# Ranks of the second sort's last four parts made in layer 0 instead of the sort, and 392 late scatters for 256, in a graph network kernel

## The chip, the cores and the metric

One core of a Trainium2 chip. The metric is the device time of one execution in microseconds: the median of three runs is 8976.88 us (8976.27 to 8980.71). Below, "POOL" is GpSimd, "DVE" VectorE, "ACT" ScalarE, "PE" TensorE and "SP" SyncE.

## The reference, cut to what matters

The reference runs four graph layers over 6250 nodes of 128 features and 100,000 edges (src, dst), each followed by a residual and a layer norm:

```
x = layernorm(x + L0(x))    mean of x[src] by dst, two 128x128 products, rows scaled to length 1
x = layernorm(x + L1(x))    (x @ weight[type])[src] * edge_weight, summed by dst, relu
x = layernorm(x + L2(x))    5 rounds: segment_sum((h @ W)[src], dst), then a GRU cell; then two dense layers
x = layernorm(x + L3(x))    an MLP on (x[src], x[dst], edge_attr) for each edge, summed by src, MLP on nodes
```

Layers 0 to 2 sum over edges by dst, layer 3 sums by src. So the edges are needed in two orders.

## The kernel before, in words

The work stands in five blocks, one after the other, each with a program for every engine and a barrier at its end: `sort_edges`, `layer0`, `layer1`, `layer2` (five rounds) and `edge_mlp` (layer 3).

**The sort.** Edges lie as 128 partitions by 784 columns. The first order (by dst, for layers 0 to 2) is made by a sorting network of 146 compare stages between 20 turns (numbers 0 to 19), in which the data are transposed, by PE and copies of ACT, alternately to rows (even turns) and to chunks (odd turns). DVE compares and moves (lines 844 to 883), ACT keeps copies (lines 543 to 557). The second order (by src, for layer 3) is a counting sort. For each of 8 parts of 98 columns, DVE makes the rank of each edge inside its tile: ten *rank turns* of five tiles (`rank_turn`, lines 781 to 814), each an equality against five tile numbers (L791), a scan (L793) and five predicated copies (L801); the last turn of a part also turns ranks into row numbers (L805 to L812) and raises `rows_done`. Ten rank turns are made ahead of the network. The others, 70 of 80, stand in the network's turns, four to each (`RANKS_A_TURN`), where DVE would else wait for the transposes.

POOL scatters the edge records (18 numbers each) to the DRAM table `slots2` in the second order, one column of 128 records by one indirect DMA (L474), in groups of eight with four small copies ahead of them (L468 to L471). A group waits for the part it belongs to. There are `NOW` = 528 such columns in the sort. The last `LATE` = 256 columns are late: ACT packs their records with their row numbers (`put_late`, lines 499 to 513) in network turn 18, SP stores them to DRAM (L426), and the later layers read them back and scatter them behind their gathers (`Late.load`, `Late.scatter`, L1081): 10 in layer 1, 46 in each of the first four rounds of layer 2, 62 in its last round. Layer 3 reads `slots2` and waits for all of them.

**Layers 0 to 2.** `gather_rows` on POOL fetches 128 rows of one chunk with one indirect DMA (L1027) into a ring of 32 chunks: 782 of them in layer 0 and layer 1, 688 in each round. SP relays (`relay_rows`): it raises `landed` for PE when four chunks have arrived, and `freed` for POOL (L1046) when PE has summed those that held the ring's places. `turns` runs a body for each 32 visits: 26 turns and one more, the first three and the last ones written out, turns 3 to 24 a loop. A body is two groups (b = 0, 1) of four halves (n = 0 to 3). For a half, PE multiplies four chunks with one-hot matrices (L1100) two halves deep in PSUM, DVE adds the four sums to their tiles (L1141) and builds the next one-hots (L1120). Between the halves stands the work of a finished tile: in layer 0 the mean (L1473 to L1476), products on PE, an ACT copy (L1374), square and sum on DVE (L1481 to L1483), a store of rows by ACT (L1370). Before the adds of each half DVE reads four column numbers into registers (L983). At the end of layer 0 POOL scatters 96 columns of counts (L1275).

In each round of layer 2 POOL waits for the previous round's stores, gathers 688 chunks, and scatters its late columns; the round's last tiles are finished by PE, DVE and ACT meanwhile. SP loads the late records of a round before it relays (L1074), once all scatters before have landed.

Of the kernel before, what the change touches and what calls it, by code (L numbers as in the profile page):

```python
# [26 lines left out]
PART = 98  # L27
# [15 lines left out]
LATE_PIECES = 7  # L43
# [43 lines left out]
REC_LATE = REC2 + 1  # L87


LATE = 256  # L90
LATE_LAYER0, LATE_LAYER1, LATE_ROUND, LATE_LAST = 0, 10, 46, 62
assert LATE_LAYER0 + LATE_LAYER1 + 4 * LATE_ROUND + LATE_LAST == LATE
# [62 lines left out]
def tables(nc, c):  # L155

    def dram(name, shape, dt=F32):
# [8 lines left out]
        late=dram("late", (SLOT, LATE * REC_LATE)),  # L166
# [109 lines left out]
def sort_edges(nc, K, T, scattered, src, dst, edge_attr, edge_type, edge_weight):  # L276
# [3 lines left out]
    with ExitStack() as c:  # L280
# [47 lines left out]
        late_all = sb("late_all", [L, LATE, REC_LATE])  # L328
        signs = late_all[:].rearrange("p c w -> p (c w)")[:, 0:FIVE * C].rearrange("p (n c) -> p n c", n=FIVE)
# [38 lines left out]
        late_made, late_out, visits_in = sem("late_made"), sem("late_out"), sem("visits_in")  # L368
        blank_set, blanked = sem("blank_set"), sem("blanked")
# [8 lines left out]
        def _(sp):  # L378
# [49 lines left out]
            sp.wait_ge(late_out, 16)  # L428
# [3 lines left out]
        def _(pool):  # L432
# [44 lines left out]
            for h in range(2):  # L477
                pool.wait_ge(scattered[h], 16 * NOW // 2)

        @block.scalar  # L480
        def _(act):
# [17 lines left out]
            def put_late(piece):  # L499

                low = C - LATE
                if piece == 0:
                    act.wait_ge(attr_in, 64)
                    act.wait_ge(rows_done, PARTS)
                    act.copy(late_all[:, :, 0].bitcast(I32), key_i[0][:, low:C]).then_inc(late_made, 1)
                elif piece == 1:
                    act.copy(late_all[:, :, 1], lane[:, low:C]).then_inc(late_made, 1)
                elif piece == 2:
                    act.copy(late_all[:, :, REC2].bitcast(I32), row[:, low:C]).then_inc(late_made, 1)
                else:  # L510
                    n = LATE // (LATE_PIECES - 3)
                    at = (piece - 3) * n
                    act.copy(late_all[:, at:at + n, 2:REC2], attr[:, low + at:low + at + n, :]).then_inc(late_made, 1)
# [6 lines left out]
            for what, n, k, level in network():  # L520
# [18 lines left out]
                else:  # L539
# [16 lines left out]
                    if rows and turn == LAST_TURN - 1:  # L556
                        put_late(6 - (k.bit_length() - 1))
# [46 lines left out]
        def _(dve):  # L604
# [456 lines left out]
class Late:  # L1061
# [6 lines left out]
    def load(self, sp, n):  # L1068

        if n == 0:  # L1070
            return
        if self.read > 0:
            sp.wait_ge(self.done, 16 * self.read)
        sp.dma_start(self.K["late_rec"][:, 0:n, :].rearrange("p c w -> p (c w)"),  # L1074
                     self.T["late"][:, self.read * REC_LATE:(self.read + n) * REC_LATE]).then_inc(self.loaded, 16)
        self.read += n

    def scatter(self, pool, n, nth):
        pool.wait_ge(self.loaded, 16 * nth)
        for c in range(n):  # L1080
            pool.indirect_dma_start(  # L1081
                out=self.T["slots2"],
                out_offset=bass.IndirectOffsetOnAxis(ap=self.K["late_rec"][:, c, REC2:REC_LATE].bitcast(I32), axis=0),
                in_=self.K["late_rec"][:, c, 0:REC2], in_offset=None).then_inc(self.done, 16)
# [116 lines left out]
def layer0(nc, K, T, late, x, w_l, b_l, w_r, rel_weight):  # L1201
# [3 lines left out]
    with c:  # L1205
# [32 lines left out]
        far_ps_ok, far_step = sem("far_ps_ok"), sem("far_step")  # L1238
        KEY_KEPT, KEYS_SORTED, RUNS_COUNTED, CHAINED, RUNS_ENDED = 4, 18, 21, 29, 35
# [16 lines left out]
        def _(sp):  # L1256
# [6 lines left out]
            relay_rows(nc, sp, K, S, 0)  # L1263
            sp.wait_ge(stored, 16 * TILES)

# [129 lines left out]
        def _(dve):  # L1395
# [62 lines left out]
            def body(turn):  # L1458
                if turn.first == 2:
                    count_far()  # L1460
                for b in range(2):
                    now, back = columns_of_places(nc, dve, DVE, K, turn, b)
                    for n in range(4):
# [5 lines left out]
                        if n == 0 and now is not None:  # L1469
# [7 lines left out]
                                              ALU.mult).then_inc(mean_ok, 1)  # L1477
                        if n == 2 and now is not None:
# [28 lines left out]
            dve.sem_inc(S.added, CREDIT)  # L1507
# [1054 lines left out]
```

## Time and profile before

| | |
|---|---|
| median of three runs | 8976.88 us |
| the profiled execution, its own time | 8970.01 us |
| its span on the core | 8968.3 us |
| busy: PE, DVE, ACT, POOL | 6261.0, 5543.9, 2571.2, 6507.7 us |
| sort block | 0 to 987.6 us |
| layer 0 | 987.6 to 2119.0 us |
| layer 1 | 2119.0 to 3117.7 us |
| layer 2 | 3117.7 to 7889.1 us |
| layer 3 | 7889.1 us to the end |

The borders are read from the first instruction of each block in the timeline. POOL is busy for 73% of the span and issues 0.95 us indirect DMAs about 1.25 us apart in every block. No engine is busy throughout, so the shares alone don't say what a change is worth: each block has to be read by itself, from what ends last in it.

### The profile page before, as it was taken

The numbers are of one execution on the slowest core, as the hardware profiler recorded it, in microseconds if no ns is written. First come the engines' busy times: TensorE is split into PE (matmuls) and PEld (weight loads), VectorE is DVE, ScalarE is ACT, GpSimd is POOL, SyncE is SP. The second block draws the span as 40 slices with busy tenths as digits, with TensorE's granted clock in tenths as the row PEclk, the third lists the DMA queues.
The fourth block names the chain that finished last, engine by engine and source line by source line (L and its number), as shares of the span: only waits on it lengthen the run. The fifth ranks groups of instructions, "written<-read, shape, count | busy, mean of one in ns | idle before, by whom it ended". The sixth has DMA issues, their size and how long they took to land. (4 is left out here: it accounts for less than half of the span.)

```text
span 8968.3 us, 161529 instructions
## 1 busy us (share of the span) xinstructions
PE 6261.0 (70%) x36545; PEld 5381.8 (60%) x36546; DVE 5543.9 (62%) x13908; ACT 2571.2 (29%) x6581; POOL 6507.7 (73%) x7005
## 2 busy tenths in 40 slices
PE   0011255552444488888888888878888999989998
PEld 0000133332333377776777677767776888878887
DVE  9999444542444466665666566656665677656666
ACT  4223111112333211121111111111112333456666
POOL 1777777776777777776777677767776777767776
PEclk9999866665555599999999999999999999999999
DMA  4000122222222244434444344434443444322223
GB/s 154 7 7 18 53 80 77 78 71 60 60 60 59 67 143 139 138 112 133 139 138 136 111 138 138 138 107 139 138 139 101 138 137 136 95 56 63 64 64 53
DMA packets 428100, 870.71 MB, mean 97 GB/s; under 512 B 117433, under 2 KB 229680, under 8 KB 427349
## 3 DMA queue, kind: packets, MB, share of 16 engines
q0 software_dynamic: 269952, 615.62, 25.6%
q10 hardware_dynamic: 122250, 189.76, 6.3%
q1 hardware_dynamic: 35529, 61.49, 2.1%
q14 instruction: 269, 2.20, 0.1%
q8 instruction: 100, 1.64, 0.1%
HBM read 763.02 MB, written 103.40 MB: 97 GB/s over the span
## 5 line engine op out<-in xcount | busy, mean ns | idle before, releaser
L1027 POOL DMA_INDIRECT rows<-state_table,rec x3440 | 3280.7, 954 | 1140.5 <-issue 1109.7
L1100 PE MATMUL l_prod<-rows,onehot 128*125 x10728 | 2625.5, 398 | 1180.0 <-SPq L1041 524.1
L1141 DVE TENSOR_TENSOR agg<-agg,l_prod 125x256 f32 (+2 forms) x5364 | 2038.6, 380 | 2111.9 <-PE l_prod L1100 1080.7
L1100 PEld LDWEIGHTS l_prod<-rows,onehot 128*125 128x125 f32 x10728 | 2000.8, 222 | 1607.0 <-issue 1412.2
L2316 POOL DMA_INDIRECT w_area<-xcol_table,l_slots x832 | 785.8, 944 | 302.0 <-issue 251.4
L1027 POOL DMA_INDIRECT rows<-rel_table,rec x782 | 738.6, 945 | 255.7 <-issue 237.7
L1027 POOL DMA_INDIRECT rows<-in_x_dram,rec x782 | 739.0, 945 | 254.2 <-issue 230.6
L1837 PE MATMUL l_prod<-l_sources,rec 125*125 125x256 f32 x3000 | 696.0, 383 | 27.3 <-DMA rec<-dense_table 25.8
L474 POOL DMA_INDIRECT slots_table<-rec_stage,row_stage x528 | 550.8, 1043 | 161.8 <-issue 143.4
L1837 PEld LDWEIGHTS l_prod<-l_sources,rec 125*125 125x125 f32 x3000 | 563.4, 190 | 121.4 <-DMA rec<-dense_table 30.6
L1792 PE MATMUL l_rh<-state,w_area 128*128 x4000 | 582.1, 279 | 3.0 <-DVE l_u L2124 3.0
L1792 PEld LDWEIGHTS l_rh<-state,w_area 128*128 128x128 f32 x4000 | 558.2, 197 | 30.8 <-issue 3.8
L1792 PE MATMUL l_nz<-l_w_t,w_area 128*128 128x125 f32 x4000 | 535.5, 275 | 0.0
L1792 PEld LDWEIGHTS l_nz<-l_w_t,w_area 128*128 128x128 f32 x4000 | 507.6, 192 | 11.6
L1120 DVE TENSOR_TENSOR onehot<-l_rest,rec 128x500 f32<-128x500 f32 x743 | 498.0, 671 | 0.0
L2115 DVE TENSOR_TENSOR agg<-agg,l_prod 125x256 f32 x750 | 316.0, 421 | 276.5 <-issue 169.1
L1973 ACT ACTIVATE l_gr<-l_rh,b_rz 128x125 f32<-128x125 f32 x250 | 91.6, 366 | 1048.6 <-PE l_rh L1792 1020.0
L1962 ACT COPY l_w_t<-agg 125x256 f32 x250 | 101.2, 405 | 950.8 <-issue 373.5
L599 PE MATMUL turned<-ident,rec 112*128 112x112 f32 x140 | 31.4, 399 | 451.7 <-DVE rec L878 410.2
L1978 ACT ACTIVATE l_gz<-l_nz,b_rz 128x125 f32<-128x125 f32 x250 | 91.6, 366 | 875.0 <-PE l_nz L1792 871.6
L1792 PE MATMUL l_rh<-l_w_t,w_area 128*128 128x125 f32 x2000 | 318.2, 283 | 0.4
L2458 DVE TENSOR_TENSOR state<-state,l_sum_ps 128x125 f32 x832 | 237.6, 286 | 123.8 <-PE l_sum_ps L2364 36.7
(427 smaller groups left out, 10299.1 us busy)
## 6 DMA issues: line engine op xcount, KB each, us to landing
rec<-dense_table ACTq DMA_DIRECT2D x125, 732.4 KB
rows<-state_table,rec POOLq DMA_INDIRECT x3440
l_sources<-state_table ACTq DMA_DIRECT2D x125, 250.0 KB
rel_table<-l_relrow ACTq DMA_DIRECT2D x50, 500.0 KB
state_table<-l_row ACTq DMA_DIRECT2D x200, 125.0 KB
dense_table<-late_rec SPq DMA_DIRECT2D x50, 366.2 KB
w_area<-xcol_table,l_slots POOLq DMA_INDIRECT x832
rows<-in_x_dram,rec POOLq DMA_INDIRECT x782, 2.5
```

Source lines behind the costliest of these rows:

```text
L474: pool.indirect_dma_start(out=T["slots2"], out_offset=bass.IndirectOffsetOnAxis(ap=row_stage[:, h, r:r + 1], axis=0), in_=rec2_stage[:, h ...
L1027: pool.indirect_dma_start(out=K["rows"][:, r, 0:width], out_offset=None, in_=table, in_offset=bass.IndirectOffsetOnAxis(ap=K["rec"][:, wor ...
L1100: last = pe.matmul(slots[k][0:LANES, 0:width], K["onehot"][:, h % ONEHOTS, k, :], rows[:, bass.ds(at[k], width)], start=True, stop=True)
L1120: dve.tensor_tensor(K["onehot"][:, q], numbers[:, None, 0:LANES].to_broadcast([128, HALF, LANES]), K["rec"][:, 1, cols, None].to_broadcast ...
L1141: dve.tensor_tensor(into, into, of, ALU.add).then_inc(S.added, 1)
L1792: last = pe.matmul(b[:, s, 0:LANES], weight[:, n % 2, out], of[n % 2], start=(n == 0), stop=(n == len(pairs) - 1))
L1837: last = pe.matmul(slots[j][0:LANES, :], counts[:, q, at:at + LANES], sources[:, q, :], start=(q == 0), stop=(q == 1))
L1962: act.copy(agg_row.rearrange("p (s n) -> p s n", s=2), agg[0:LANES, :, bass.ds(col, SLOT)]).then_inc(taken, 1)
L1973: act.activation(gr[:, 0, 0:LANES], r_b[:, 0, 0:LANES], ACT.Sigmoid, bias=K["b_rz"][:, 0:1])
L2115: dve.tensor_tensor(sums, sums, of, ALU.add).then_inc(dadded, 1)
L2316: pool.indirect_dma_start(out=gathered[:, q, k * D:(k + 1) * D], out_offset=None, in_=T["xcol"], in_offset=bass.IndirectOffsetOnAxis(ap=sl ...
L2458: dve.tensor_tensor(a, a, sum_ps[:, k * LANES:(k + 1) * LANES], ALU.add).then_inc(added, 1)
```

## The change

- The sort ranks and scatters `NOW` = 392 columns, four parts of eight. `LATE` is 392, four whole parts. DVE makes 40 rank turns there, not 80.
- At the end of the sort POOL copies the bucket and spare numbers of the last 392 columns, and the tile bases, to `w_area` (three copies).
- ACT packs the late records without row numbers, in two passes of 196 columns, six copies each: in network turns 16 and 18. SP stores each pass.
- Layer 0's DVE program is written out (27 bodies, no loop), and in each group of turns 4 to 23, after the adds of half n = 1, it makes one rank turn: 40 in all. Its operands lie in SBUF (`rank` and the tile numbers were in PSUM). At the end SP stores the 392 columns of row numbers to `late_rows`.
- `Late.load` reads records and row numbers by two DMAs. The late scatters are 16 in layer 1, 63 in each of four rounds, 62 in the last round, and a second batch of 62 after it, which is loaded when the first has landed.

```diff
-LATE = 256
-LATE_LAYER0, LATE_LAYER1, LATE_ROUND, LATE_LAST = 0, 10, 46, 62
+LATE = 392
+LATE_LAYER1, LATE_ROUND, LATE_LAST = 16, 63, 62
+RANK_TILES = 5
+RANK_TURNS = TILES // RANK_TILES
+FIRST_RANKED = 4
...
@@ sort_edges, sync
-            sp.wait_ge(late_made, LATE_PIECES)
-            sp.dma_start(T["late"], late_all[:].rearrange("p c w -> p (c w)")).then_inc(late_out, 16)
+            for n in range(LATE_PASSES):
+                sp.wait_ge(late_made, (n + 1) * LATE_PIECES)
+                sp.dma_start(T["late"][:, n * AT_ONCE * REC2:(n + 1) * AT_ONCE * REC2],
+                             late_area[:, 0:AT_ONCE * REC2]).then_inc(late_out, 16)
...
@@ sort_edges, gpsimd
             for h in range(2):
-                pool.wait_ge(scattered[h], 16 * NOW // 2)
+                pool.wait_ge(scattered[h], 16 * SC_HALF * ((NOW // SC_HALF + 1 - h) // 2))
+            pool.tensor_copy(K["late_bucket"], bucket[:, NOW:C]).then_inc(late_kept, 1)
+            pool.tensor_copy(K["late_row"], spare[:, NOW:C]).then_inc(late_kept, 1)
+            pool.tensor_copy(K["late_base"], base[:]).then_inc(late_kept, 1)
+            pool.wait_ge(late_kept, 3)
...
@@ sort_edges, scalar
-                    if rows and turn == LAST_TURN - 1:
-                        put_late(6 - (k.bit_length() - 1))
+                    if rows and turn in (LAST_TURN - 3, LAST_TURN - 1) and k > 1:
+                        put_late((turn - LAST_TURN + 3) // 2, 7 - k.bit_length())
...
@@ sort_edges, vector
-                    turns_now = min(ranked + RANKS_A_TURN, PARTS * TILES // FIVE)
+                    turns_now = min(ranked + RANKS_A_TURN, NOW // PART * TILES // FIVE)
...
@@ Late
         sp.dma_start(self.K["late_rec"][:, 0:n, :].rearrange("p c w -> p (c w)"),
-                     self.T["late"][:, self.read * REC_LATE:(self.read + n) * REC_LATE]).then_inc(self.loaded, 16)
+                     self.T["late"][:, self.read * REC2:(self.read + n) * REC2]).then_inc(self.loaded, 16)
+        sp.dma_start(self.K["late_rows"][:, 0:n], self.T["late_rows"][:, self.read:self.read + n])\
+            .then_inc(self.loaded, 16)
...
@@ layer0, sync
             relay_rows(nc, sp, K, S, 0)
+            sp.wait_ge(rows_done, LATE_PARTS)
+            sp.dma_start(T["late_rows"], K["late_bucket"].bitcast(I32)).then_inc(rows_out, 16)
             sp.wait_ge(stored, 16 * TILES)
+            sp.wait_ge(rows_out, 16)
...
@@ layer0, vector
+                        if n == 1 and 0 <= 2 * (turn.first - FIRST_RANKED) + b < LATE_PARTS * RANK_TURNS:
+                            rank_turn(2 * (turn.first - FIRST_RANKED) + b)
...
+                dve.tensor_copy(is_tile[:, :, 0], K["late_base"][:, tiles])
+                step(dve.tensor_tensor(is_tile[:, :, 1:PART + 1], bucket[:, None, :].to_broadcast(part),
+                                       K["iota_row"][:, tiles][:, :, None].to_broadcast(part), ALU.is_equal))
+                step(dve.tensor_tensor_scan(rank.rearrange("p n c -> p (n c)"), carry.rearrange("p n c -> p (n c)"),
+                                            is_tile.rearrange("p n c -> p (n c)"), 0.0, ALU.mult, ALU.add))
...
-            turns(dve, 0, body)
+            for i in range(TURNS + 1):
+                body(Turn(dve, 0, i), rank_turn)
...
@@ layer2, sync
             late.load(sp, LATE_LAST)
             relay_rows(nc, sp, K, S, LAST, NEAR, NEAR_VISITS)
+            late.load(sp, LATE_LAST)
...
@@ layer2, gpsimd
                 late.scatter(pool, LATE_ROUND if rnd < LAST else LATE_LAST, 2 + rnd)
+            late.scatter(pool, LATE_LAST, 2 + rounds)
```

## Rows read from the trace of the kernel before

**Rows 1.** The page's head.
```profile
span 8968.3 us, 161529 instructions
```
**Rows 2.** Windows: us, busy of PE, PEld, DVE, ACT, POOL, clock, DMA share.
```profile
170.00:988.00 818.00, 66.06 (x281) 51.27 (x280) 733.38 (x1629) 207.19 (x366) 613.64 (x795) 1.00 0.07 15
988.00:2120.00 1132.00, 561.53 (x2323) 398.93 (x2323) 523.00 (x1745) 193.51 (x553) 831.41 (x879) 0.67 0.25 72
```
**Rows 3.** Timeline of POOL at the end of the sort: start, duration.
```profile
977.69 0.96 POOL L474 DMA_INDIRECT slots_table<-rec_stage,row_stage  x1 [0.30 <-issue]
987.59 0.15 POOL L1268 MEMSET rows<- 128x32 f32 x1 [8.95 <-POOLq L146]
```
**Rows 4.** Timeline of DVE, its last instruction in the sort.
```profile
932.26 0.25 DVE L897 TENSOR_SCALAR w_area<-sort_key 128x96 int32<-128x96 int32 x1
```
**Rows 5.** POOL's drain at the end of the sort block (line 280): ns, start.
```profile
L280 POOLq DRAIN  x1: 6608/6608/6608, 980.1 to 980.1; - x1
```
**Rows 6.** Timeline of DVE: the ten rank turns of the first part.
```profile
170.52 0.21 DVE L787 COPY src_row<-spare 128x98 f32<-128x98 f32 x1
171.00 0.17 DVE L790 COPY is_tile<-base 128x5 f32<-128x5 f32 x1
...
201.41 0.26 DVE L805 TENSOR_TENSOR src_row<-src_row,other_row 128x98 f32<-128x98 f32 x1
202.93 0.26 DVE L812 SCALAR_TENSOR_TENSOR src_row<-tmp,slot_f 128x98 f32<-128x98 f32 x1
```
**Rows 7.** Timeline of DVE in network turns 18 and 19, which hold no ranks.
```profile
868.98 0.63 DVE L864 TENSOR_TENSOR swap<-rec 112x448 f32<-112x448 f32 x1 [2.56 <-ACT rec L525]
871.65 0.67 DVE L869 COPY_PREDICATED rec<-swap,rec 112x448 f32<-112x448 int32 x1 [2.04 <-ACT rec L548]
896.65 0.52 DVE L869 COPY_PREDICATED sort_key<-swap,sort_key 128x272 f32<-128x272 int32 x1 [1.63 <-ACT rec L548]
```
**Rows 8.** POOL in the sort: all 528 scatters by line, and the 50th group's start.
```profile
L474 POOL DMA_INDIRECT slots_table<-rec_stage,row_stage x528 | 550.8, 1043 | 161.8 <-issue 143.4 <-POOL row_stage L471 15.6 <-DMA slots_table<-rec_stage,row_stage 2.8
...
786.19 0.21 POOL L468 COPY rec_stage<-dst_i 128x8 int32<-128x8 int32 x1
```
**Rows 9.** Timeline of DVE in layer 0: one square, and then the next group.
```profile
1704.29 0.29 DVE L1481 TENSOR_TENSOR l_sq<-l_o 125x128 f32<-125x128 f32 x1 [1.42 <-ACT l_o L1374]
...
1719.60 1.57 DVE L1141 TENSOR_TENSOR agg<-agg,l_prod 125x130 f32 x4 [1.45 <-PE l_prod L1100]
...
1723.98 0.29 DVE L1481 TENSOR_TENSOR l_sq<-l_o 125x128 f32<-125x128 f32 x1 [2.22 <-ACT l_o L1374]
...
1726.75 1.57 DVE L1141 TENSOR_TENSOR agg<-agg,l_prod 125x130 f32 x4 [1.97 <-issue]
```
**Rows 10.** DVE's loads of column numbers to registers: ns min/median/max.
```profile
L983 DVEq TENSOR_LOAD <-visits x1341: 335/344/1887, 1025.9 to 7789.5; - x192
```
**Rows 11.** Waits of POOL from 990 to 1982 us: total, times, longest.
```profile
POOL rows L1027 <- SPq L1046: 23.6, 26, 3.5
```
**Rows 12.** Timeline in the sort: a scan and the scatter beside it.
```profile
461.56 1.20 DVE L793 TENSOR_TENSOR_SCAN rank<-carry,is_tile 128x495 f32<-128x495 f32 x1
462.02 1.49 POOL L474 DMA_INDIRECT slots_table<-rec_stage,row_stage  x1 [0.30 <-issue]
```
**Rows 13.** Timeline of POOL: late scatters, and the first gather after them.
```profile
3108.66 0.96 POOL L1081 DMA_INDIRECT slots_table<-late_rec  x1 [0.30 <-issue]
...
4062.96 0.97 POOL L1027 DMA_INDIRECT rows<-state_table,rec  x1 [23.09 <-issue]
...
5946.43 0.97 POOL L1027 DMA_INDIRECT rows<-state_table,rec  x1 [20.43 <-issue]
...
7892.19 0.97 POOL L2316 DMA_INDIRECT w_area<-xcol_table,l_slots  x1 [48.77 <-DMA l_slots<-slots_table]
```
**Rows 14.** DMA issues: size, us to landing.
```profile
late_rec<-late_table SPq DMA_DIRECT2D x1, 589.0 KB, 3.9
```
**Rows 15.** Timeline of SP at the start of layer 3.
```profile
7889.15 0.80 SPq L2271 DMA_DIRECT2D l_slots<-slots_table  x2
```

More of the change, by code:

```diff
@@ L42 @@
 LOW_BITS = (1 << LANE_BIT) - 1
-LATE_PIECES = 7
+LATE_PIECES, LATE_PASSES = 6, 2
 assert ROWS * ROWS_BLOCKS == COLS
@@ L165, in tables @@
         state=[dram("state0", (NODES, STATE)), dram("state1", (NODES, STATE))],
-        late=dram("late", (SLOT, LATE * REC_LATE)),
+        late=dram("late", (SLOT, LATE * REC2)), late_rows=dram("late_rows", (SLOT, LATE), I32),
         xcol=dram("xcol", (NODES, D)),
@@ L1456, in count_far, with body @@
                 dve.sem_inc(cells_ok, 1)
-            def body(turn):
+            def body(turn, rank_turn):
                 if turn.first == 2:
@@ L1507, in _, with scratch @@
             dve.sem_inc(S.added, CREDIT)
+            def scratch(at, n):
+                return K["code_block"][:, at:at + n]
+            many = RANK_TILES * (PART + 1)
+            is_tile, rank, carry = (a.rearrange("p (n c) -> p n c", n=RANK_TILES)
+                                    for a in (scratch(0, many), scratch(many, many), K["late_carry"]))
+            other_row, slot_f, low_f = (scratch(2 * many + k * PART, PART) for k in range(3))
+            slot_i, low_i = (scratch(2 * many + k * PART, PART).bitcast(I32) for k in range(3, 5))
@@ new lines, in rank_turn @@
+            def rank_turn(turn):
+                q, t = divmod(turn, RANK_TURNS)
+                step = Steps(dve, rank_step, 2 + q * (RANK_TURNS * 2 + 7) + t * 2 + (1 if t > 0 else 0))
+                row, bucket = (K[n][:, q * PART:(q + 1) * PART] for n in ("late_row", "late_bucket"))
+                part = [SLOT, RANK_TILES, PART]
+                tiles = slice(t * RANK_TILES, (t + 1) * RANK_TILES)
+                if t == 0:
+                    step(dve.memset(other_row, 0.0))
+                dve.tensor_copy(is_tile[:, :, 0], K["late_base"][:, tiles])
[3 more added lines that the diff above has]
+                                            is_tile.rearrange("p n c -> p (n c)"), 0.0, ALU.mult, ALU.add))
+                dve.tensor_copy(K["late_base"][:, tiles], rank[:, :, PART])
+                for n in range(RANK_TILES):
+                    place = turn * RANK_TILES + n
+                    if place > 1:
+                        dve.wait_ge(row_set, place - 1)
+                    dve.copy_predicated(other_row if place % 2 else row, is_tile[:, n, 1:PART + 1].bitcast(I32),
+                                        rank[:, n, 1:PART + 1]).then_inc(row_set, 1)
+                dve.wait_ge(row_set, (turn + 1) * RANK_TILES)
+                if t == RANK_TURNS - 1:
+                    step(dve.tensor_tensor(row, row, other_row, ALU.add))
+                    step(dve.tensor_copy(low_i, row))
+                    step(dve.tensor_scalar(slot_i, low_i, 7, None, ALU.arith_shift_right))
+                    step(dve.tensor_scalar(low_i, low_i, SLOT - 1, None, ALU.bitwise_and))
+                    dve.tensor_copy(slot_f, slot_i)
+                    step(dve.tensor_copy(low_f, low_i))
+                    step(dve.scalar_tensor_tensor(bucket.bitcast(I32), low_f, float(PITCH), slot_f, ALU.mult, ALU.add))
+                    dve.sem_inc(rows_done, 1)
@@ L2514, in gnn @@
         K["far_key"] = K["w_area"][:, 4 * BLOCKS:4 * BLOCKS + FAR]
+        at = 4 * BLOCKS + FAR
+        for name, n in (("late_bucket", LATE), ("late_row", LATE), ("late_base", TILES),
+                        ("late_carry", RANK_TILES * (PART + 1))):
+            K[name] = K["w_area"][:, at:at + n]
+            at += n
         K["code_block"], K["weight_block"] = (K["w_area"][:, k * 2 * BLOCKS:(k + 1) * 2 * BLOCKS] for k in range(2))
```

50 lines of the change are left out of this document (29 added, 21 removed).

## The prediction, on record before the changed kernel ran

> **What bounds the kernel now.** I read the span first [rows 1], then the busy times block by block [rows 2], then each block's end in the timelines. The reader is to see that no engine fills any block, so every block has to be asked what ends last in it. In the sort DVE is busy for 733 of 818 us and POOL for 614, yet it is POOL that ends it: its last scatter stops at 978.65 and the next block begins at 987.59 [rows 3], while DVE had done its last instruction at 932.51 [rows 4]. The end of the block behind POOL's last scatter costs 8.95 us, most of it POOL's own drain of 6.6 us [rows 5]. In layers 0 and 1 POOL's chain of gathers sets the end; in layer 0 it is held up by the ring only for 23.6 us in all [rows 11]. In a round of layer 2 POOL gathers, scatters its late columns and then waits 20 to 23 us for the round's stores [rows 13]: that wait is the room for more late scatters. Between the last scatter of layer 2 and layer 3 POOL is idle for 48.77 us [rows 13]. So the change moves scatters from a place where they are on the path to places with room, and must pay for ranks that DVE now makes beside layer 0's gathers.
>
> **The sort.** POOL loses 136 of 528 scatters. The start of its 50th group, at 786.19 [rows 8], is where its 392 columns end; with the landing of the last one, three copies of at most a few us (392 numbers a lane) and the 6.6 us drain it is ready before 800, well ahead of DVE. DVE becomes what ends the block. It loses 40 rank turns: ten take 201.41 - 171.00 = 30.4 us, so one takes 3.04 us, 40 take 121.6. Each part also has a head of 0.48 us (170.52 to 171.00) and a tail of 1.78 (201.41 to 203.19) [rows 6]: four times 2.3 is 9.2. Together 130.8 us. But the ranks covered waits for the transposes. Of the 20 network turns, 0 to 6 keep their four ranks and 7 keeps two, so 8 to 17 are left bare. What a bare turn costs stands in turns 18 and 19: 2.56 + 2.04 = 4.60 us for a turn to rows, 1.63 for one to chunks [rows 7]. Five of each: 23.0 + 8.2 = 31.2. Gain: 130.8 - 31.2 = 99.6 us. DVE's end moves from 932.5 to 832.9, and with some 1.2 us of barrier (987.59 less the end of POOL's drain, 986.7, and DVE's own drain) layer 0 starts at 834.1 instead of 987.6: **-153.5 us**. Bounds: if bare turns cost nothing -184, if they cost twice as much -122; I take the rows, since turns 18 and 19 are the same code. ACT's second pass of packing goes into turn 16, between its copies for the network, as the one pass in turn 18 does, where DVE shows no wait for it: 0, covered by ACT's idle time; without that cover it would be some 6 us. The stores of both passes end before DVE: 0.
>
> **Layer 0.** A rank turn comes after the one-hots of half 1. There DVE now waits 1.45 us for PE, adds half 2, and waits 2.22 us for ACT's copy of the product [rows 9]: 3.67 us idle between. The turn needs 3.04, and the register load that was hidden in the first wait now stands behind it, 0.34 [rows 10] and 0.2 of issue: 3.6. So the adds of half 2 come 2.2 us later, which PE doesn't need before it is two halves on, and the square starts when it did. In the group before it the square waited only 1.42 [rows 9]; there some 0.8 us is late. Next behind the square is the wait of 1.97 us before half 3 [rows 9], a register load that takes up to 1.9 us against a median of 0.34 [rows 10]; it lies beside ACT's store of the tile's rows, and I expect it to end when that transfer does, whenever it starts, which swallows up to 1.4 us. The four tails of 1.8 us may cost 1 us each. On the DVE side 0 to 4 us.
>
> POOL's side is the open one. A scatter beside a scan took 1.49 us, where one alone takes 0.96 [rows 3, 12]: 0.54 more. The 528 scatters average 1043 ns against 0.96 [rows 3, 8], about 0.085 x 528 = 45 us too much, over 70 rank turns that stood beside them: 0.65 us each if all is put on the ranks. Forty such turns cost POOL 26 us. The ring's waits are 23.6 us [rows 11]; a POOL that is delayed elsewhere doesn't wait there, because the consumer frees the places at its own pace. That leaves **+3 us**. Bounds: below, 0, or -5 if the written-out program frees places sooner (the loop's register arithmetic falls away); above, see the second rival. The GPSIMD Engine Reference of the Trainium skill ("Key points") says that GpSimd shares its SBUF interfaces with VectorE and contends with "two SBUF inputs". The row of the scan, which reads two SBUF operands, agrees with its 1.49 us. By the rule alone the equality and the predicated copies, which get a second SBUF operand by this change, would hold POOL too, which is the second rival below. The 96 count scatters and the block's end are as before; the store of row numbers lies beside them: 0. SP's new wait for `rows_done` stands behind its whole relay, and the last part is ranked in turn 23 of 26: nobody waits.
>
> **Layer 1.** Six more late scatters of 0.96 + 0.30 = 1.26 us [rows 13], behind the last gather and ahead of POOL's drain, on the path: **+7.6 us**.
>
> **Rounds 1 to 4.** 17 more each: 21.4 us. The first idle time is 23.09, the shortest of the three others 20.43, of which 0.30 stays: nothing in the first, at most 1.3 in each of the others, say 1.0: **+3.0 us**, between 0 (if PE sets the pace of a round anyway) and 10 (if the scatters slow the last stores). The late records' load on SP has to wait for scatters that now land 21 us later; its relay stands behind that. The scatters land about when the stores do, and the first relay is due only when four new gathers have landed, over 5 us later: 0, at worst 2 us each.
>
> **The end of layer 2.** The first 62 scatters end at 7892.19 - 48.77 = 7843.4 as before. Then: landing 2.1; SP issues the load, 0.5; 3.9 to its landing [rows 14], and 0.5 for the second, small DMA; 62 x 1.26 = 78.1; that gives 7928.5. Behind it POOL's landing and drain, 8.95 less the 0.9 of barrier [rows 3], then 0.9, then 3.04 from SP's first load of layer 3 to the first gather (7889.15 to 7892.19) [rows 13, 15]. That is 7940.4, against 7892.2: **+48.2 us**; from 42 (landing and load in 2 us) to 55.
>
> **Sum.** -153.5 + 3 + 7.6 + 3.0 + 48.2 = -91.7. The profiled execution took 8970.0 us by its own time (span 8968.3), so 8878 there; the median of the three runs lies 6.9 us above it, so **8885 us**.
>
> **Rivals.**
> 1. *As summed*: 8885, own range 8872 to 8899. Chance 0.66.
> 2. *POOL is held by more of the rank turn*. The scan is 1.20 of a rank turn's 3.04 us. If the whole turn, now all from SBUF, delays POOL as the scan does (0.54 in 1.20) [rows 12], a turn costs 1.37, forty 55, less the waits of 23.6: +31 for +3, so 8913. For it: all operands are in SBUF now. Against it: a part of the 45 us belongs to network stages. 0.14.
> 3. *The ranks are partly exposed* in DVE's chain, 0.5 to 1.5 us a turn, where PE waits for the adds: +20 to +60, 8905 to 8945. The idle time fits so narrowly that any shift of PE's pace opens it. 0.07.
> 4. *Slower*: the ranks stand wholly in series in layer 0. Place: half 1 to half 2 of each group, where PE and DVE take turns; price 130.8 us, giving 8885 - 3 + 131 = 9013. It decides against the change from (91.7 + 3)/40 = 2.4 us of 3.3 us a turn. The two idle times of 1.45 and 2.22 [rows 9] speak against it. A second way to the same end is DVE starving on its written-out program, but in the sort it runs one without gaps. 0.04.
> 5. *Better*: the consumer of layer 0 gets faster without loop arithmetic and frees the ring earlier, or bare network turns cost less: down to 8865. 0.09.
>
> That the change doesn't do what it says I can exclude from the code but for counts, which the profile will show.
>
> **How the numbers follow.** Rivals 1, 2, 5 and most of 3 are faster. A measurement of this kernel can tell 0.2%, 18 us, from no change: within it fall a corner of 3 and partly exposed cases between 3 and 4. Range: 8866 to 8922.
>
> **What would show it.** In the sort 392 scatters that end near 790, DVE's last instruction near 833 and layer 0's first near 834; bare turns with DVE waits of 4.6 and 1.6. In layer 0 rank turns of 3.04 us, `l_sq` waiting for ACT for under 0.5 us, POOL's gathers above 945 ns in the mean and its waits for `freed` under 10 us, and a length of 1131 + 3. Idle times before the rounds of 1.6, then 0.3; a scatter train of 78 us behind a pause of 7 us at the end of layer 2. A layer 0 longer by over 30 us, or bare turns of 8 us, would make the sum wrong.

## The result, and the profile of the changed kernel

The changed kernel takes 8923.1 us in the median of 4 runs (8919.8 to 8927.5), the kernel before 8976.6 on the same chips: ratio 0.9941, 95% interval 0.9928 to 0.9954. It is faster, but by 53.5 us where 91.7 were forecast, and 1 us outside the range. The profiled execution took 8924.76 us (span 8923.1), against 8970.0 (span 8968.3) [rows 1]: 45.2 us of span gained. Ten of the runs below (groups one, three and five) met a condition of the chip in which the kernel before itself takes 11,547 to 11,696 us, so only the durations of single instructions are read from them, and no times.

I cut both traces at the same five borders: start of layer 0, of layer 1, of layer 2 and of layer 3 (always POOL's first instruction of the block, or its first gather), and the end. Windows of the kernel before; the columns are those of [rows 2], the last of them being GB/s:
```profile
0.00:987.59 987.59, 70.32 (x296) 54.99 (x297) 888.77 (x1876) 302.79 (x520) 623.86 (x814) 1.00 0.15 43
987.59:2119.81 1132.22, 561.53 (x2323) 398.93 (x2323) 523.11 (x1746) 193.91 (x553) 831.56 (x881) 0.67 0.25 72
2119.81:3118.47 998.66, 445.74 (x1746) 370.26 (x1746) 434.69 (x1351) 310.44 (x1045) 748.24 (x792) 0.53 0.24 64
3118.47:7892.19 4773.72, 4166.02 (x24600) 3655.62 (x24600) 2990.84 (x7180) 1099.79 (x3223) 3518.29 (x3686) 0.96 0.45 129
7892.19:8968.30 1076.11, 1017.40 (x7580) 902.02 (x7580) 706.47 (x1758) 664.24 (x1240) 785.79 (x832) 0.96 0.26 62
```
The same windows of the changed kernel:
```profile
0.00:832.23 832.23, 70.21 (x296) 55.01 (x297) 762.60 (x1480) 304.84 (x525) 459.62 (x613) 0.93 0.17 50
832.23:1969.89 1137.66, 575.24 (x2323) 411.04 (x2323) 643.09 (x2140) 193.88 (x553) 852.61 (x881) 0.65 0.25 72
1969.89:2982.73 1012.84, 449.30 (x1746) 373.90 (x1746) 434.33 (x1351) 310.60 (x1045) 760.32 (x798) 0.53 0.23 63
2982.73:7840.60 4857.87, 4182.17 (x24600) 3667.93 (x24600) 2985.92 (x7180) 1099.85 (x3223) 3673.77 (x3816) 0.95 0.44 128
7840.60:8923.10 1082.50, 1014.86 (x7580) 895.93 (x7580) 700.34 (x1758) 662.40 (x1240) 791.84 (x832) 0.97 0.26 61
```
Differences of the first column: sort -155.4, layer 0 +5.4, layer 1 +14.2, layer 2 +84.2 (of which 40.3 up to the end of the first late batch at 7748.00, 43.8 behind it), layer 3 +6.4. The odd one is the last: the change touches nothing in layer 3, and POOL alone, with 832 instructions in both, is busy there for 6.0 us more. The same in layer 1, where six scatters more account for 7.6 of 14.2. So the next view is one instruction by line: minimum, median and maximum in ns. Before, scatters in the sort, cell scatters (the 96 columns of counts) of layer 0, and gathers of layer 1:
```profile
L474 POOL DMA_INDIRECT slots_table<-rec_stage,row_stage x528: 954/958/3405, 206.9 to 977.7; - x176
L1275 POOL DMA_INDIRECT dense_table<-l_count,l_cell_i x96: 954/958/1120, 1981.5 to 2101.7; - x96
L1027 POOL DMA_INDIRECT rows<-rel_table,rec x782: 940/944/1067, 2119.8 to 3096.0; - x196
```
The changed kernel, its scatters in the sort, the same cell scatters, and its gathers:
```profile
L483 POOL DMA_INDIRECT slots_table<-rec_stage,row_stage x392: 954/958/3406, 206.9 to 770.6; - x196
L1293 POOL DMA_INDIRECT dense_table<-l_count,l_cell_i x96: 963/967/1005, 1830.8 to 1951.7; - x96
L1041 POOL DMA_INDIRECT rows<-state_table,rec x3440: 949/953/1437, 2982.7 to 7667.2; - x192
L1041 POOL DMA_INDIRECT rows<-rel_table,rec x782: 947/952/1071, 1969.9 to 2951.7; - x196
```
In the sort a scatter has the median of before, 958. From layer 0 on every indirect DMA of POOL is 7 to 9 ns longer, the minimum as much as the median: cell scatters 967 for 958, gathers of layer 1 952 for 944. The 305 ns between two of them are unchanged. These instructions are the same word for word in both programs. Over 6000 of them at 7 to 9 ns would be what is missing. The few instructions of POOL that are new stand right where the step is (timeline of POOL in the changed kernel):
```profile
770.65 0.96 POOL L483 DMA_INDIRECT slots_table<-rec_stage,row_stage  x1 [0.30 <-issue]
773.19 0.51 POOL L488 COPY w_area<-bucket 128x392 f32<-128x392 f32 x1 [1.58 <-DMA slots_table<-rec_stage,row_stage]
773.64 0.51 POOL L489 COPY w_area<-spare 128x392 f32<-128x392 f32 x1
774.10 0.22 POOL L490 COPY w_area<-base 128x50 f32<-128x50 f32 x1
832.23 0.15 POOL L1286 MEMSET rows<- 128x32 f32 x1 [57.91 <-POOLq L150]
```
The three copies take 1.1 us and are followed by 57.9 us of waiting at the block's barrier, for DVE. Nobody waits for them. They were costed at nothing.

### The profile page after: what moved, and what is told of

It reads as the page before. It is cut to its first block and busy times, and to the rows that moved or that the text cites. A ratio compares the mean times of both kernels' runs of the same rounds, so it can differ in the third digit from the quotient of the medians.

```text
span 8923.1 us, 160142 instructions
## 1 busy us (share of the span) xinstructions
PE 6291.8 (71%) x36545; PEld 5403.8 (61%) x36546; DVE 5526.3 (62%) x13906; ACT 2571.6 (29%) x6586; POOL 6538.2 (73%) x6940
## 5 line engine op out<-in xcount | busy, mean ns | idle before, releaser
L1041 POOL DMA_INDIRECT rows<-in_x_dram,rec x782 | 759.5, 971 | 238.5 <-issue 237.0
L483 POOL DMA_INDIRECT slots_table<-rec_stage,row_stage x392 | 404.3, 1031 | 120.3 <-issue 106.6
L1095 POOL DMA_INDIRECT slots_table<-late_rec,late_rows x392 | 382.9, 977 | 127.3 <-issue 121.9
L1703 ACT ACTIVATE onehot<-onehot,rec 128x125 f32<-128x125 f32 x832 | 263.0, 387 | 162.1 <-issue 85.8
```

Of the source, the lines that this page charges most:

```text
L483: pool.indirect_dma_start(out=T["slots2"], out_offset=bass.IndirectOffsetOnAxis(ap=row_stage[:, h, r:r + 1], axis=0), in_=rec2_stage[:, h ...
L1041: pool.indirect_dma_start(out=K["rows"][:, r, 0:width], out_offset=None, in_=table, in_offset=bass.IndirectOffsetOnAxis(ap=K["rec"][:, wor ...
L1095: pool.indirect_dma_start(out=self.T["slots2"], out_offset=bass.IndirectOffsetOnAxis(ap=self.K["late_rows"][:, c:c + 1], axis=0), in_=self ...
L1703: last = act.activation(oh, oh, ACT.Copy, scale=K["rec"][:, 3, turn.column(h * HALF + k, 1)])
```

## The experiments

There are five groups of runs. In the second and the fourth, from which times are read, the kernel before took 8975.1 (14 runs) and 8977.2 (7 runs). A run that puts copies into the kernel before also gives their results places in `w_area`, which is left out of the code below; nothing reads them. The measure I use is **cell scatters less sort scatters**, both of the same program: 958 - 958 = 0 before, 967 - 958 = 9 in the changed kernel.

**First group: what makes the step.** Candidates: the copies (theory A), the count of scatters in the sort (B), addresses (C: the change widens a buffer, and each later one lies 64 bytes higher).

The kernel before, with the copies:
```diff
             for h in range(2):
                 pool.wait_ge(scattered[h], 16 * NOW // 2)
+            pool.tensor_copy(K["late_bucket"], bucket[:, C - 392:C]).then_inc(late_kept, 1)
+            pool.tensor_copy(K["late_row"], spare[:, C - 392:C]).then_inc(late_kept, 1)
+            pool.tensor_copy(K["late_base"], spare[:, 0:TILES]).then_inc(late_kept, 1)
+            pool.wait_ge(late_kept, 3)
```


> The kernel before, with three GpSimd copies of 392, 392 and 50 numbers a lane and their wait put behind the sort's last scatter, as the changed kernel has them; nothing reads what they write. In the changed kernel every indirect DMA from layer 0 on takes 8 to 9 ns longer than before (gathers 944 to 952 ns in the median, cell scatters 958 to 967), in the sort none does. Theory A, the copies are the last instructions GpSimd runs ahead of some 6000 indirect DMAs and leave it in a state that costs each 8 ns: gathers of layer 0 have a median of 952 here, and the kernel takes about 9020 us (5900 x 8 ns = 47 more than 8970, copies 2). Rivals B (number of scatters in the sort) and C (addresses moved by 64 bytes): 944 and about 8973.

Measured: sort 958, cell scatters 967, gathers 952. The step is there.

The changed kernel, with the copies on ACT:
```diff
-            pool.tensor_copy(K["late_bucket"], bucket[:, NOW:C]).then_inc(late_kept, 1)
-            pool.tensor_copy(K["late_row"], spare[:, NOW:C]).then_inc(late_kept, 1)
-            pool.tensor_copy(K["late_base"], base[:]).then_inc(late_kept, 1)
-            pool.wait_ge(late_kept, 3)
...
+            act.wait_ge(rows_done, NOW // PART)
+            act.copy(K["late_bucket"], bucket[:, NOW:C]).then_inc(late_kept, 1)
+            act.copy(K["late_row"], spare[:, NOW:C]).then_inc(late_kept, 1)
+            act.copy(K["late_base"], base[:]).then_inc(late_kept, 1)
+            act.wait_ge(late_kept, 3)
             act.wait_ge(moved, 5 * STAGES)
```


> The changed kernel with the same three copies made by ScalarE in the sort, so that GpSimd's last instructions there are scatters. Theory A (state left by the copies): gathers back to 944 ns, time about 8923 - 43 = 8880 us. Rivals B (number of scatters) and C (addresses): 952 ns and 8923.

Measured: sort 962, cell scatters 962, gathers 947. No step, but the whole program, its sort too, 3 to 4 ns higher, which no theory had foreseen.

Count and addresses, each in the kernel before:
```diff
-LATE = 256
-LATE_LAYER0, LATE_LAYER1, LATE_ROUND, LATE_LAST = 0, 10, 46, 62
+LATE = 264
+LATE_LAYER0, LATE_LAYER1, LATE_ROUND, LATE_LAST = 0, 18, 46, 62
...
```


> The kernel before with 520 scatters in the sort instead of 528 (65 batches of 8, an odd number as the changed kernel's 49) and 264 late ones, the 8 in layer 1. Rival B, the count or its parity decides GpSimd's state: gathers at 952 ns and about 9015 us. Theory A and rival C: 944 ns; the sort 10 us shorter or the same, layer 1 10 us longer, about 8970.

```diff
-                ("late_rec", [128, max(LATE_LAYER0, LATE_LAYER1, LATE_ROUND, LATE_LAST), REC_LATE]))
+                ("late_rec", [128, max(LATE_LAYER0, LATE_LAYER1, LATE_ROUND, LATE_LAST), REC_LATE]),
+                ("shift", [128, 16]))
```


> The kernel before with a buffer of 16 unused numbers a lane behind the late records, which moves every later buffer by 64 bytes, as in the changed kernel. Rival C, the addresses: gathers at 952 ns and about 9017 us. Theory A and rival B: 944 ns and 8970.

Measured: both 958 in the sort, 958 for cell scatters and 944 for gathers. B and C fall.

**Second group: times, and is it the program or the day?** The 3 to 4 ns of the run above asked for a control: perhaps each loading of a program draws its own offset, and the difference between the kernels was such a draw (D). The first two are the kernels unchanged.

> The kernel before, unchanged, profiled once more. The four runs ahead of this one were on a chip on which the kernel before takes 11,696 us, so their times don't compare with 8970; their medians of one instruction do. There the kernel before plus three GpSimd copies gathered at 952 ns and its two siblings without copies at 944. Theory A (the copies leave a state): 944 ns here, about 8975 us. Rival D (each loading of a program draws its own offset of a few ns, and the difference between before and changed kernel was such a draw): any value from 942 to 952.

> The changed kernel, unchanged, profiled once more. Theory A: gathers at 952 ns, 8923 us. Rival D: another offset than before, and with 944 ns a time near 8880.

> The changed kernel with the three copies made by ScalarE in the sort, once more. In the run ahead its sort scatters took 962 ns in the median and its gathers 947, so the copies' absence took 5 ns from the gathers and something else put 4 on the scatters. Theory A: gathers 944 to 947, and about 8923 - 5900 x (5 to 8 ns) = 8876 to 8893 us. Rival D: no fixed relation; 952 ns and 8923 us are as likely.

> The kernel before with the three copies behind its last scatter, once more. Theory A: 952 ns, and about 8975 + 47 = 9020 us. Rival D: any value from 942 to 952, and 8973 with 944.

Measured: the kernel before 8974.3 us (8 runs), ratio 0.9999 (0.9989 to 1.0009); this profile has the raised level, 962 in the sort and 962 in layer 0. The changed kernel 8917.1 (2 runs), 0.9938 (0.9918 to 0.9958), 958 and 967. **Copies on ACT: 8880.9 us (8878.3 to 8885.3, 4 runs), ratio 0.9899, interval 0.9883 to 0.9916.** The kernel before with copies: 9010.0 (3 runs), ratio 1.0042 (1.0026 to 1.0058), 35 us slower than without, where 45 to 47 were expected. The same two lines of the run with the copies on ACT:
```profile
L1294 POOL DMA_INDIRECT dense_table<-l_count,l_cell_i x96: 954/958/998, 1827.1 to 1947.1; - x96
L1042 POOL DMA_INDIRECT rows<-rel_table,rec x782: 940/944/1012, 1965.3 to 2940.8; - x196
```
and of the kernel before with three copies:
```profile
L475 POOL DMA_INDIRECT slots_table<-rec_stage,row_stage x528: 952/958/3406, 207.0 to 978.0; - x176
L1280 POOL DMA_INDIRECT dense_table<-l_count,l_cell_i x96: 963/967/1005, 1985.6 to 2106.5; - x96
```
Put in, the copies bring the step and cost 35 us; taken out, they take it away and give 36 to 42 back (8917.1 and 8923.1 less 8880.9). Theory A stands. D is right that an offset of 3 to 4 ns comes and goes, but that lifts a whole program, sort and all, and doesn't make the step.

**Third group: what about the copies.** All are the kernel before; M says the count matters, W the width, P the place.
```diff
+            pool.tensor_copy(K["late_bucket"], bucket[:, C - 392:C]).then_inc(late_kept, 1)
+            pool.wait_ge(late_kept, 1)
```


> The kernel before with one GpSimd copy (392 numbers a lane) behind the sort's last scatter. With three, every later indirect DMA took 8 to 9 ns more. Measure: median of the 96 cell scatters of layer 0 less the median of the sort's scatters, 0 in the kernel before (958, 958; 962, 962) and 9 with three copies (967, 958). Theory M, the number of GpSimd's data instructions counts by some small cycle (those of the sort come in fours, so three more put it out of step): 0 or a value between, not surely 9. Theory W, a wide copy leaves the state: 9. Theory P, a copy behind the last scatter, of whatever size and number: 9.

The next one with a fourth copy behind the first group's three:
```diff
             pool.tensor_copy(K["late_base"], spare[:, 0:TILES]).then_inc(late_kept, 1)
-            pool.wait_ge(late_kept, 3)
+            pool.tensor_copy(K["late_more"], spare[:, 0:TILES]).then_inc(late_kept, 1)
+            pool.wait_ge(late_kept, 4)
```


> The kernel before with four GpSimd copies (392, 392, 50, 50) behind the last scatter. Theory M: in step again, difference 0, time about 8976. Theories W and P: 9 ns and about 9010 us.

```diff
+            pool.tensor_copy(K["late_bucket"][:, 0:8], bucket[:, C - 392:C - 384]).then_inc(late_kept, 1)
+            pool.tensor_copy(K["late_row"][:, 0:8], spare[:, C - 392:C - 384]).then_inc(late_kept, 1)
+            pool.tensor_copy(K["late_base"][:, 0:8], spare[:, 0:8]).then_inc(late_kept, 1)
+            pool.wait_ge(late_kept, 3)
```


> The kernel before with three GpSimd copies of 8 numbers a lane each behind the last scatter. Theory W: 0 and 8975 us. Theories M and P: 9 ns and about 9010 us.

```diff
             for n in range(NOW // SC_HALF):
...
+                if n == 50:
+                    pool.tensor_copy(K["late_bucket"], bucket[:, C - 392:C]).then_inc(late_kept, 1)
+                    pool.tensor_copy(K["late_row"], spare[:, C - 392:C]).then_inc(late_kept, 1)
+                    pool.tensor_copy(K["late_base"], spare[:, 0:TILES]).then_inc(late_kept, 1)
+                    pool.wait_ge(late_kept, 3)
```


> The kernel before with the three wide copies (392, 392, 50) ahead of the 51st of 66 batches of the sort. Theory M: the scatters of the last 16 batches already take 9 ns more than those of the first 50 and so does all behind. Theory W: the same, unless the batch's own small copies undo it. Theory P, the place behind the last scatter: 0 everywhere, about 8978 us (copies 2 to 3 us).

Measured, sort and cell scatters: one copy 958, 967; four 962, 971 (the raised level again, and the step on top of it); three tiny ones 958, 967; early 958, 958. Neither count nor width: one copy is enough, and so are three of 8 numbers (M and W fall). Ahead of sixteen more batches, which have copies of their own, they do nothing.

**Fourth group: kind, barrier, and a repair that leaves the copies on POOL.**
```diff
+            pool.tensor_copy(K["late_bucket"][:, 0:8].bitcast(I32), spare[:, 0:8]).then_inc(late_kept, 1)
+            pool.wait_ge(late_kept, 1)
```


> The kernel before with one converting copy (8 numbers a lane, float to integer) behind the sort's last scatter, where a plain copy cost every later indirect DMA 9 ns. Measure: cell scatters of layer 0 less the sort's scatters. Theory P, the place behind the last scatter: 9. Theory T, the kind of the last data instruction (the sort's batches end in a converting copy, and the difference there is 0): 0.

```diff
+            pool.memset(K["late_bucket"], 0.0).then_inc(late_kept, 1)
+            pool.wait_ge(late_kept, 1)
```


> The kernel before with one memset (392 numbers a lane) behind the last scatter. Theory P: 9 ns. Theory T: 0 or another value, as layer 0 begins with memsets too, in both kernels, and those alone do nothing.

```diff
             pool.iota(trash_i[:], pattern=[[SLOT, FAR]], base=CELLS + CELL_AT, channel_multiplier=1)\
                 .then_inc(trash_made, 1)
+            pool.tensor_copy(K["late_bucket"][:, 0:8], K["zeros"][:, 0:8]).then_inc(copy_made, 1)
+            pool.wait_ge(copy_made, 1)
```


> The kernel before with one plain copy of 8 numbers in layer 0, behind its iota and ahead of its first gather, and none in the sort. Theory T (a plain copy is the last data instruction ahead of thousands of indirect DMAs): 9 ns. Theory P (behind the last scatter of the sort, ahead of the block's drain): 0.

```diff
                 pool.wait_ge(rows_done, -(-(n + 1) * SC_HALF // PART))
+                if n == NOW // SC_HALF - 1:
+                    pool.tensor_copy(K["late_bucket"], bucket[:, NOW:C]).then_inc(late_kept, 1)
+                    pool.tensor_copy(K["late_row"], spare[:, NOW:C]).then_inc(late_kept, 1)
+                    pool.tensor_copy(K["late_base"], base[:]).then_inc(late_kept, 1)
+                    pool.wait_ge(late_kept, 3)
...
-            pool.tensor_copy(K["late_bucket"], bucket[:, NOW:C]).then_inc(late_kept, 1)
-            pool.tensor_copy(K["late_row"], spare[:, NOW:C]).then_inc(late_kept, 1)
-            pool.tensor_copy(K["late_base"], base[:]).then_inc(late_kept, 1)
-            pool.wait_ge(late_kept, 3)
```


> The changed kernel with its three copies on GpSimd as before, but ahead of the last of the 49 batches. If what matters is that a batch's own copies and scatters follow them, difference 0, gathers of 944 ns and, on a chip where the changed kernel takes 8920, a time of 8881 us, as with the copies on ScalarE (8880.9). If the copies' cost came from standing anywhere near the end, 9 ns and 8920.

Measured, cell scatters: converting copy 967, and 9017.0 us; memset 958, 8966.7; copy in layer 0 967, 9010.3 (these three times are single runs); and the copies ahead of the last batch 958, **8882.6 us (8879.7 to 8888.9, 4 runs), ratio 0.9897 (0.9881 to 0.9914)**, all against 8977.2. So T falls on the converting copy. P fails in part: its 9 ns for the memset and its 0 for the copy in layer 0, which stands behind the block's barrier and costs the same, were both wrong. The memset also settles a rival that none of the letters names, the place of POOL's later instructions: it lengthens POOL's program by one instruction and one wait, as the one copy does, and there is no step. Cell scatters of the run with the copy in layer 0, of the one with the memset, and of the one with the copies ahead of the last batch:
```profile
L1278 POOL DMA_INDIRECT dense_table<-l_count,l_cell_i x96: 963/967/1005, 1983.5 to 2104.3; - x96
L1278 POOL DMA_INDIRECT dense_table<-l_count,l_cell_i x96: 954/958/997, 1979.4 to 2099.4; - x96
L1294 POOL DMA_INDIRECT dense_table<-l_count,l_cell_i x96: 954/958/1072, 1828.3 to 1948.4; - x96
```

In POOL's program the copy in layer 0, with its wait, is all that differs from before (timeline of POOL):
```profile
987.49 0.21 POOL L1271 IOTA l_trash_i<- 128x96 int32 x1
987.64 0.19 POOL L1273 COPY w_area<-zeros 128x8 f32<-128x8 f32 x1
988.23 1.00 POOL L1028 DMA_INDIRECT rows<-in_x_dram,rec  x1 [0.40 <-POOL w_area L1273]
```
0.19 us of work, and 33 us in the time of that one run. And the repaired order, with the last of the three copies, which takes as long as before, and the batch's own behind it:
```profile
761.36 0.22 POOL L478 COPY w_area<-base 128x50 f32<-128x50 f32 x1
761.64 0.20 POOL L482 COPY rec_stage<-dst_i 128x8 int32<-128x8 int32 x1
...
762.13 0.19 POOL L485 CAST row_stage<-src_row 128x8 int32<-128x8 f32 x1
762.60 1.40 POOL L488 DMA_INDIRECT slots_table<-rec_stage,row_stage  x1 [0.28 <-POOL row_stage L485]
```

**Fifth group: the batch's own copies once more.** Is it what is copied (O), or the sequence of the four (S)?
```diff
+            pool.tensor_copy(row_stage[:, h, :], row[:, cols]).then_inc(late_kept, 1)
+            pool.wait_ge(late_kept, 1)
```


> The kernel before with the last batch's converting copy (row numbers into their stage, 8 numbers a lane) made a second time behind the last scatter, same operands. Measure: cell scatters of layer 0 less the sort's scatters. Theory P (a copy behind the last scatter, whatever it copies): 9 ns, about 9010 us. Theory O (its operands or place in memory decide: those of the batches are harmless): 0, 8975 us. Theory S (the sequence of the four decides): 9.

```diff
+            pool.tensor_copy(rec2_stage[:, s, 0].bitcast(I32), key_i[0][:, cols]).then_inc(late_kept, 1)
+            pool.tensor_copy(rec2_stage[:, s, 1], lane[:, cols]).then_inc(late_kept, 1)
+            pool.tensor_copy(rec2_stage[:, s, 2:REC2], attr[:, cols, :]).then_inc(late_kept, 1)
+            pool.tensor_copy(row_stage[:, h, :], row[:, cols]).then_inc(late_kept, 1)
+            pool.wait_ge(late_kept, 4)
```


> The kernel before with all four copies of the last batch made a second time behind the last scatter, and no scatters after them. Theory P: 9 ns. Theories O and S: 0, since the same four copies stand ahead of every batch of the sort, whose scatters take 958.

Measured: sort 959, cell scatters 968; and 958, 967. Both have the step of 9. O and S fall: the very copies that do no harm 66 times in the sort do it when they stand between the sort's last scatter and layer 0's first gather.

What the runs show, then: one to four copies by POOL, plain or converting, of 8 to 392 numbers a lane, right behind the last scatter of the sort or right ahead of the first gather of layer 0, make the indirect DMAs that follow, 6188 in the kernel before, 7 to 9 ns longer in the minimum and the median, to the end of the kernel 8 ms later. The last batch's eight scatters between the copy and layer 0 prevent it, a memset doesn't cause it. All 20 profiles fall in line: the 11 with such a copy have the step, the 9 without have none.

**What goes on inside POOL stays open**: that the sort's scatters take 958 behind copies (in all 20 profiles only the first of a batch is longer, by 20 ns in the median, and the other seven are not), and those of layer 0 don't return to it in thousands, is not explained by any theory that I had. One reading was not separated from the place: in every case with the step the first indirect DMA behind the copy is a gather, in every case without it, it is a scatter. Whether a single scatter there would be enough, or a copy in the middle of a layer's gathers would do harm, was not tried.

## Why the prediction was wrong, point by point

The windows of the run with the copies on ACT (same columns, same borders) tell the step of the copies from all other terms:
```profile
0.00:832.25 832.25, 70.21 (x296) 55.00 (x297) 762.66 (x1480) 305.83 (x528) 458.31 (x611) 0.90 0.17 50
832.25:1965.31 1133.06, 571.43 (x2323) 408.10 (x2323) 645.96 (x2140) 193.85 (x553) 848.07 (x882) 0.65 0.25 72
1965.31:2971.61 1006.30, 446.51 (x1746) 371.43 (x1746) 435.28 (x1351) 310.39 (x1045) 753.73 (x798) 0.52 0.23 63
2971.61:7800.28 4828.67, 4178.54 (x24600) 3666.55 (x24600) 2990.68 (x7180) 1099.79 (x3223) 3645.50 (x3816) 0.95 0.44 128
7800.28:8876.60 1076.32, 1013.30 (x7580) 894.18 (x7580) 701.70 (x1758) 662.55 (x1240) 785.41 (x832) 0.97 0.26 62
```

| us against the kernel before | forecast | changed kernel | copies on ACT |
|---|---|---|---|
| sort | -153.5 | -155.4 | -155.3 |
| layer 0 | +3 | +5.4 | +0.8 |
| layer 1 | +7.6 | +14.2 | +7.6 |
| layer 2 to the end of the first late batch | +3.0 | +40.3 | +11.7 |
| behind it, to layer 3 | +48.2 | +43.8 | +43.2 |
| layer 3 | 0 | +6.4 | +0.2 |
| sum (span) | -91.7 | -45.2 | -91.7 |

**The step that failed** is in the paragraph on the sort: "three copies of at most a few us", costed with what they take and hidden behind DVE. They are hidden. The premise beneath the whole sum, that an indirect DMA of layers 0 to 3 costs after the change what the rows of before show, is what broke. Its price is the difference of the last two columns: 4.6 us in layer 0, 6.6 in layer 1, 28.6 in layer 2 up to the end of the first late batch, 0.6 behind it, and 6.2 in layer 3, 46.5 in all. It can be worked out from the medians: 782 gathers x 8 ns = 6.3 in layer 1, 832 x 8 = 6.7 in layer 3, 3440 x 7 ns + 314 late scatters x 9 = 26.9 in layer 2. In layer 0 the same sum gives 7.1, and only 4.6 were measured. In the medians of the runs' times the step costs 35 to 42 us. Without it the forecast of 8885 stands against 8880.9 and 8882.6 measured. That the sums of span agree to 0.1 us, -91.7 and -91.7, is luck: against the copies on ACT the terms miss by 9 us one way and by 2 to 5 the other, and cancel. Nor is each term good to a microsecond: the 48.77 us ahead of layer 3 [rows 13] are 43.9 in the second profile of the kernel before. No rival held this: none of them had a cost that outlives the instruction that makes it. Rival 2's 8913 lies near the result, but by another mechanism, which layer 0's +0.8 refutes. Rival 5 falls too: the bare turns waited as forecast, and layer 0 was not shorter.

**The sort** was right. The ten bare turns each waited as turns 18 and 19 had [rows 7]; one of the five of each kind, timeline of the changed kernel:
```profile
710.38 0.63 DVE L878 TENSOR_TENSOR swap<-rec 112x448 f32<-112x448 f32 x1 [2.56 <-ACT rec L539]
```
with 2.05 and 1.61 to 1.67 us behind it, as before. The last scatter ended at 771.6 (the 786.19 of [rows 8] was 15 us too late, which DVE hides), DVE's last instruction at 831.04 (forecast 832.9), layer 0 began at 832.23 (834.1).

**Layer 0**: right in the sum by two terms too large. POOL's gathers beside the ranks took 755.7 us in the run with copies on ACT, against 739.0 before: 16.7 us, or 0.42 a rank turn, not the 0.65 and 26 that I took from the sort. On the other side the waits for `freed` of 23.6 [rows 11] contained 26 ordinary pauses of 0.30, which stay; idle time ahead of the gathers fell from 254.2 to 238.5, by 15.7. 16.7 - 15.7 = 1.0, measured 0.8. Groups by line of layer 0, of the kernel before:
```profile
L1027 POOL DMA_INDIRECT rows<-in_x_dram,rec x782 | 739.0, 945 | 254.2 <-issue 230.6 <-SPq L1046 23.6
```
and of the run with the copies on ACT:
```profile
L1042 POOL DMA_INDIRECT rows<-in_x_dram,rec x782 | 755.7, 966 | 238.5 <-issue 237.3 <-SPq L1061 1.2
```
That POOL hardly waits for `freed` any more was forecast (under 10 us). DVE has the ranks in its idle time. Timeline of the changed kernel, one group as in [rows 9]:
```profile
1409.37 1.56 DVE L1155 TENSOR_TENSOR agg<-agg,l_prod 125x130 f32 x4 [0.29 <-issue]
...
1411.43 0.16 DVE L1546 COPY w_area<-w_area 128x5 f32<-128x5 f32 x1
...
1413.57 0.94 DVE L1556 COPY_PREDICATED w_area<-w_area 128x98 f32<-128x98 int32 x5
1415.10 1.56 DVE L1155 TENSOR_TENSOR agg<-agg,l_prod 125x130 f32 x4 [0.59 <-DVE w_area L1556]
...
1417.16 0.28 DVE L1501 TENSOR_TENSOR l_sq<-l_o 125x128 f32<-125x128 f32 x1
```
1411.43 to 1414.51 is 3.08 us (forecast 3.04), 0.59 of wait stand behind it, and the square follows the adds and a one-hot with no wait for ACT. Rivals 3 and 4 fall with layer 0's length. A rank turn cost POOL 0.42 us, less than the 0.54 that was read beside one scan [rows 12] and far from rival 2's 1.37. The Trainium skill ("GPSIMD Engine Reference", "Key points") names contention of GpSimd with VectorE instructions "with two SBUF inputs"; the trace doesn't bear out the reading by which every such instruction of a rank turn holds POOL as the scan did.

**The rounds** were put too low, by a lesser miss: +3.0 forecast, +11.7 with DMAs at their old price, above the bound of 10. The first of the four was as forecast (3915.09 - 2971.61 = 943.5 us against 944.5), the other three lasted 947.2, 944.7 and 944.8 us against 941.4, 942.1 and 942.0, and the fifth 956.6 against 955.0. POOL still waited 4.0, 1.5 and 2.7 us at the end of these three (I had expected 0.3), so it is the stores that came later, not the scatters that took too long. I had taken "PE sets the pace" for the gentle case. Why these rounds are 3 to 6 us longer beside 17 more scatters, I haven't tested; the unchanged kernel's own rounds differ by 3 to 4 us between its two profiles, the second of which has gathers 3 ns longer.

**The end of layer 2**: 43.2 to 43.8, inside 42 to 55, below the 48.2 forecast. The pause before the second batch was 5.3 to 5.4 us, where I had 7.0; the second batch took 81, not 78.1; and between the last scatter and layer 3 there were 5.9 us, not 11.9. POOL's drain there ended 1.7 us after the last scatter. The 11.9 were in the main taken from the sort, whose drain of 6.6 us begins 1.4 us after the last scatter [rows 5]. That it begins while scatters still run doesn't explain the difference: the drain of the kernel before at this place began 15 us ahead of the end of its last scatter and ended 7.4 us behind it:
```profile
L1700 POOLq DRAIN  x1: 22766/22766/22766, 7828.1 to 7828.1; - x1
```
Why the new one is quicker stays open. Timeline of POOL in the changed kernel:
```profile
7753.39 0.97 POOL L1095 DMA_INDIRECT slots_table<-late_rec,late_rows  x1 [5.39 <-DMA late_rows<-late_rows_table]
...
7840.60 0.98 POOL L2383 DMA_INDIRECT w_area<-xcol_table,l_slots  x1 [5.88 <-DMA l_slots<-slots_table]
```

## What to carry to other kernels

When a change leaves thousands of instructions of one kind untouched, compare their minimum and median before and after, block by block: 8 ns on over 6000 of them took some 40 of 92 us of this change's gain, no wait shows it, and in POOL's busy time it is under 1%. An instruction that is hidden, and for which nobody waits, may still set the price of what follows. In this kernel it pays to keep POOL's data copies ahead of its last batch of scatters, or to give them to ScalarE. Either makes it faster than both kernels given here: 8882.6 and 8880.9 us. That other kernels with long trains of indirect DMAs behind a copy gain by the same is not shown, but it is cheap to look for.

## What the runs showed of the hardware that was not expected

- The step itself, as above: 7 to 8 ns for gathers, 9 for scatters, after one copy of 0.19 us, for 8 ms.
- A second, independent offset: in 3 of the 20 profiles (copies on ACT in the first group, the kernel before in the second, four copies in the third) every indirect DMA of the whole program, the sort's too, took 3 to 4 ns more (962 for 958). The kernel before that was profiled with it took 8984.5 us, the longest of its 8 runs.
